# Layer normalisation moved beside a selective scan, one more drive on GpSimd, softplus summed by TensorE

## The chip, the cores and the metric

The kernel runs on one core of a Trainium2 chip. A core has five engines that run side by side, each with its own in-order stream of instructions: TensorE (PE, matrix products), VectorE (DVE), ScalarE (ACT, functions of one value), GpSimd (POOL), and SyncE (SP), which here only issues DMA transfers. They meet through semaphores. The metric is the time of one execution in microseconds on the device, the median of several. The kernel before takes 5625.2 us (three runs, 5623.45 to 5625.22).

## The reference

The input is 8 images of 96 channels and 64 x 64 pixels in float32. Two layers follow each other. The first is a 17 x 17 convolution per channel between two batch normalisations, a 96 x 96 pointwise product, GELU, and a gate per image and channel; its result is added to the input. The second is a bidirectional selective scan (Mamba). Cut to what matters:

```python
h = h * a[:, :, None, None]          # a: gate per image and channel
x = residual + gamma * h             # first layer
# second layer, tokens = the 4096 pixels of an image
mu = xh.mean(-1, keepdims=True); var = xh.var(-1, keepdims=True)
xn = (xh - mu) * rsqrt(var + 1e-05) * ln_g + ln_b
# _mamba, once forward and once over the flipped tokens
x, z = xz[..., :192], xz[..., 192:]  # xz = xn @ W_in
x = silu(causal_conv(x, 4 taps) + conv_b)
proj = x @ W_xproj                   # 6 + 16 + 16 columns
dt = softplus(proj[..., :6] @ W_dt + b_dt)
h = exp(dt * A) * h + dt * B_t * x_t # 192 channels x 16 states
y = sum_s(h * C_t) + x * D
out = (y * silu(z)) @ W_out          # forward + backward
```

## The kernel before

The program has five stages, with a barrier between them: `convolution`, `pointwise` (which leaves the ungated result in DRAM as `act_scr` and the gates in SBUF), `normalise`, `scan` and `output`.

`normalise` works in 64 slices of 512 tokens (8 images, 8 slices each), channels on the 96 partitions. Per slice VectorE makes gate x act + x, TensorE subtracts the mean with a centring matrix, ScalarE squares, TensorE averages, ScalarE makes the reciprocal root with logarithm and exponential, VectorE scales and shifts, and the slice is stored to `xn_scr`.

`scan` goes through 32 iterations of two passes. A pass is one direction of one chunk of 1024 tokens. It has 24 units, each of 128 partitions: 8 channels x 16 states. For a unit, TensorE spreads B over the partitions into one of three PSUM tiles `u_ps` (two bf16 matmuls); VectorE multiplies it by dt x (`u_rep`), the drive; ScalarE makes the decay exp(dt A) from `dt_rep`; VectorE runs the recurrence (`tensor_tensor_scan`) into `hring`; GpSimd multiplies by C into `hc`; TensorE gathers 16 states to a channel in `y_ps`, two units at a time in odd steps. For the units in `POOL_UNITS` GpSimd makes the drive from `u_rep` and `b_rep` into `drive_p`, VectorE does not, TensorE does not spread, and ScalarE puts the decay into the PSUM tile.

A pass has 24 steps, numbered m, and a written table says what each engine does in each step beside the units. The function `run` plays it to each engine in the same order. `front` at step m belongs to unit m + 8 on ScalarE, to unit m + 7 (spread and drive) on TensorE and VectorE, and to unit m + 6 for the scan. The other kinds are: `conv`, the causal convolution for the pass after next, in three groups with a ScalarE copy each (`CONV_AT`); `prep`, for the next pass: SiLU, LOW (the 38 columns of proj, `LOW_AT`), the dt products (`DT_AT`), softplus as relu(v) + ln(1 + exp(-|v|)), u = dt x (`U_AT`), and the stores and loads that replicate dt, u, B and C over the partitions through DRAM; `back`, gather and skip; `gate` and `slice`, which finish one slice of 512 tokens per pass of the image before: z (`Z_AT`), the sum of the two directions in two parts (`SUM_Y_AT`), gating by VectorE, projection (`PROJECT_AT`), result (`RES_AT`). All of conv, prep, gate and slice share one PSUM tile, `prep_ps`, so they follow each other strictly: every product in it waits until the one before is copied out. In softplus the two parts are added by GpSimd (`SUM_AT`), and GpSimd multiplies u.

`output` finishes the last image.

## Time and profile before

| | us |
|---|---|
| median of three runs | 5625.2 |
| the profiled execution | 5622.07 |
| its span, first to last instruction | 5620.2 |
| VectorE busy | 5265.8 (94%) |
| GpSimd busy | 4899.0 (87%) |
| TensorE busy | 4417.3 (79%) |
| ScalarE busy | 3184.7 (57%) |

The stages can be told from the busy time in slices of the span: convolution up to about 340 us, pointwise to 460, `normalise` 460 to 617, `scan` from there to about 5575, then `output`. Lines of the profile are lines of the kernel before: L1419 is the scan, L1401 the drive multiply, L1464 the multiplication by C, L1451 GpSimd's drive, L1170 the spread, L1188 the gather, L1199 the skip, L1211 and L1214 the convolution groups, L1227 and L1230 LOW, L1267 and L1268 the y sum, L1273 and L1274 the projection, L1434 gating, L691 the scaling in `normalise`. A float32 product is recorded as two matmul instructions. The mean of one instruction contains some 0.1 us of overlap with the next one on its engine, so rows in order of time, read from start to start, give what it costs in a dense sequence. TensorE's granted clock (PEclk) is a share of 2.4 GHz and takes two levels, 1.2 and 2.4 GHz, so 0.50 and 1.00.

### The profile page before, as it was taken

How to read it: one execution, taken by the hardware profiler on the slowest of the kernel's cores; microseconds unless marked ns; L12 is line 12 of the kernel's file. 1: busy time of each engine (PE TensorE's matmuls, PEld its weight loads, DVE VectorE, ACT ScalarE, POOL GpSimd, SP SyncE). 2: the span in 40 equal slices, each digit the busy share in tenths (PEclk: the TensorE clock that was granted, in tenths of full speed). 3: DMA queues.
4: the chain of work that ended last, by engine and by line, in shares of the span. 5: the costliest groups of instructions: out<-in, count | busy, mean ns of one | idle time of the engine just before them, and what ended most of it. 6: DMA issues, size and time to landing. Idle time of an engine off the chain costs nothing. (4 is left out here: it accounts for less than half of the span.)

```text
span 5620.2 us, 74988 instructions
## 1 busy us (share of the span) xinstructions
PE 4417.3 (79%) x17412; PEld 1176.0 (21%) x17412; DVE 5265.8 (94%) x3821; ACT 3184.7 (57%) x5221; POOL 4899.0 (87%) x2361
## 2 busy tenths in 40 slices
PE   6878577778878787788887887878778887788887
PEld 4553111111111111111111111111111111111111
DVE  5556499999999999999999999999999999999997
ACT  2237455555555566555666555665555566655564
POOL 0020299999999999999999999999999999999998
PEclk9999776667777777777777777777777777777777
DMA  2238555556656556666656665666665665666666
GB/s 75 76 92 241 164 189 184 186 183 200 212 191 202 196 196 197 207 193 209 191 194 196 204 204 198 196 196 197 202 208 189 206 194 194 198 206 198 205 193 200
DMA packets 365955, 1062.74 MB, mean 189 GB/s; under 512 B 71396, under 2 KB 119926, under 8 KB 315340
## 3 DMA queue, kind: packets, MB, share of 16 engines
q1 hardware_dynamic: 355724, 1045.89, 57.8%
q10 hardware_dynamic: 8064, 14.16, 0.8%
q0 software_dynamic: 1984, 1.06, 0.1%
q14 instruction: 166, 1.36, 0.1%
q8 instruction: 17, 0.28, 0.0%
HBM read 849.20 MB, written 211.63 MB: 189 GB/s over the span
## 5 line engine op out<-in xcount | busy, mean ns | idle before, releaser
L1464 POOL TENSOR_TENSOR hc<-hring,c_rep 128x1024 f32<-128x1024 f32 x1541 | 3599.4, 2358 | 73.1 <-DVE hring L1419 69.6
L1419 DVE TENSOR_TENSOR_SCAN hring<-decay,carry,u_ps 128x1024 f32<-128x1024 f32 x1221 | 2833.8, 2346 | 0.0
L1170 PE MATMUL u_ps<-stack_b,w_spread 48*128 48x512 bf16 x2442 | 992.4, 495 | 1008.6 <-DVE hring L1419 1003.7
L1401 DVE TENSOR_TENSOR u_ps<-u_ps,u_rep 128x1024 f32<-128x1024 f32 x1221 | 1491.7, 1222 | 69.0 <-DMA u_rep<-u_scr 52.9
L1295 ACT ACTIVATE decay<-dt_rep,w_a 128x1024 f32<-128x1024 f32 x1222 | 1396.4, 1145 | 221.2 <-DVE hring L1419 208.1
L1188 PE MATMUL y_ps<-hc,w_gather 128*32 128x512 f32 x6144 | 1131.2, 818 | 0.0
L1295 ACT ACTIVATE u_ps<-dt_rep,w_a 128x1024 f32<-128x1024 f32 x322 | 359.3, 1116 | 1104.2 <-DVE hring L1419 1103.9
L1451 POOL TENSOR_TENSOR drive_p<-u_rep,b_rep 128x1024 f32<-128x1024 f32 x322 | 759.5, 2359 | 10.7 <-DMA u_rep<-u_scr 10.7
L1419 DVE TENSOR_TENSOR_SCAN hring<-u_ps,carry,drive_p 128x1024 f32<-128x1024 f32 x321 | 755.7, 2354 | 0.0
L1170 PEld LDWEIGHTS u_ps<-stack_b,w_spread 48*128 48x128 bf16 x2442 | 144.8, 100 | 2371.0 <-DVE hring L1419 2166.7
L1211 PE MATMUL prep_ps<-xn,w_conv 128*128 128x512 f32 x792 | 476.6, 749 | 27.2 <-DMA xn<-xn_scr 25.5
L1318 ACT ACTIVATE xc<-prep_ps,w_conv_b 128x512 f32<-128x512 f32 x198 | 135.7, 685 | 410.0 <-PE prep_ps L1211 394.8
L322 DVE TENSOR_SCALAR xpad<-xraw,scale,shift 64x128 f32<-64x128 f32 (+1 forms) x600 | 184.0, 359 | 140.9 <-DMA xraw<-in_x_cols 138.1
L367 PE MATMUL pc<-xpad,toep 128*64 128x256 f32 x1920 | 253.7, 410 | 67.1 <-DVE xpad L322 67.1
L233 POOL COPY part<-wide 102x160 bf16 (+1 forms) x26 | 8.9, 343 | 322.9 <-PE pw L346 301.1
L1311 ACT COPY ends<-hring 128x1 f32<-128x1 f32 x1540 | 271.6, 176 | 0.0
L1478 POOL TENSOR_TENSOR b<-b 128x128 f32<-128x128 f32 x65 | 25.7, 395 | 256.8 <-DMA b<-bc_scr 256.8
L1188 PEld LDWEIGHTS y_ps<-hc,w_gather 128*32 128x32 f32 x6144 | 136.1, 122 | 497.8 <-issue 456.0
L1471 POOL TENSOR_TENSOR dt_sb<-soft,dt_sb 128x1024 f32<-128x1024 f32 (+1 forms) x130 | 235.6, 1813 | 3.3 <-ACT soft L1353 3.3
L1475 POOL TENSOR_TENSOR soft<-dt_sb,xa 128x1024 f32<-128x1024 f32 (+1 forms) x130 | 235.1, 1808 | 0.2
L1211 PEld LDWEIGHTS prep_ps<-xn,w_conv 128*128 128x128 f32 x792 | 172.5, 233 | 270.4 <-issue 239.5
L1199 PE MATMUL y_ps<-xa,w_skip 128*32 128x512 f32 (+1 forms) x1536 | 225.0, 662 | 0.0
(148 smaller groups left out, 4044.3 us busy)
## 6 DMA issues: line engine op xcount, KB each, us to landing
dt_rep<-dt_scr SPq DMA_DIRECT2D x194, 1024.0 KB, 5.9
u_rep<-u_scr SPq DMA_DIRECT2D x194, 1024.0 KB, 8.0
c_rep<-bc_scr SPq DMA_DIRECT2D x260, 512.0 KB, 4.9
b_rep<-bc_scr SPq DMA_DIRECT2D x130, 512.0 KB, 4.3
xn<-xn_scr SPq DMA_DIRECT2D x132, 384.0 KB, 5.4
y_scr<-y_sb SPq DMA_DIRECT2D x768, 64.0 KB, 2.0
xn<-xn_scr SPq DMA_DIRECT2D x132, 256.0 KB, 4.7
dt_scr<-dt_sb SPq DMA_DIRECT2D x260, 128.0 KB, 2.1
```

The source lines that it names most:

```text
L367: last = nc.tensor.matmul(pc[c][64 * q:64 * q + 64, 0:B * XH].rearrange("p (f b x) -> p f b x", f=2, b=B), toep[par][:, c * CELLS + k, :], ...
L1170: mm = nc.tensor.matmul(u_ps[nv % NSLOT][:, sl], w["spread"][:, q, :], upper(stack_b[drv][:, sl]), start=True, stop=True)
L1188: last = nc.tensor.matmul(y_ps[at:at + 32, :], w["gather"][:, :], hc[n % NHC][:, i * SL:(i + 1) * SL], start=(q == 0), stop=(q == QN - 1))
L1211: mm = nc.tensor.matmul(prep_ps[:, :], w["conv"][:, j, 0:P], xn[:, j, PART[g]], start=(j == 0), stop=(j == 2))
L1295: nc.scalar.activation(to[:, :], dt_rep[r][:, b, :], ACT.Exp, scale=w["a"][:, col:col + 1]).then_inc(decay_ready, 1)
L1311: nc.scalar.copy(ends[:, drv, nv:nv + 1], hring[nv % NHR][:, end:end + 1]).then_inc(kept, 1)
L1401: nc.vector.tensor_tensor(slot[:, :], slot[:, :], u_rep[r][:, b, :], ALU.mult).then_inc(drive_ready, 1)
L1419: nc.vector.tensor_tensor_scan(hring[nv % NHR][:, ::step], factor[:, ::step], term[:, ::step], carry[:, drv, nv:nv + 1], ALU.mult, ALU.add ...
L1451: nc.gpsimd.tensor_tensor(drive_p[k % 2][:, :], u_rep[r][:, b, :], b_rep[q][:, :], ALU.mult).then_inc(pool_drive, 1)
L1464: nc.gpsimd.tensor_tensor(hc[nv % NHC][:, :], hring[nv % NHR][:, :], c_rep[q][:, :], ALU.mult).then_inc(c_applied, 1)
L1471: nc.gpsimd.tensor_tensor(dt_sb[:, HALVES[h]], soft[:, HALVES[h]], dt_sb[:, HALVES[h]], ALU.add).then_inc(dt_ready, 1)
L1475: nc.gpsimd.tensor_tensor(soft[:, HALVES[h]], dt_sb[:, HALVES[h]], xa[dr][:, HALVES[h]], ALU.mult).then_inc(u_ready, 1)
```

## The change

Three things change.

1. `normalise` only does image 1 (8 slices). Images 2 to 8 are normalised inside `scan`, one slice of 512 tokens per pass, for the image after the one that is scanned (a new kind, `norm`; the last four iterations have none). There the tokens are on the partitions: TensorE centres with the gated centring matrix on act and the plain one on x (8 products of 96 columns), ScalarE squares with a row sum, makes the reciprocal root, scales, TensorE turns the four blocks back, ScalarE applies gain and bias, SP loads and stores. The slice also lives in `prep_ps`, between the result of the step before and the convolution.
2. `POOL_UNITS` has six units in place of five, every fourth.
3. The sum in softplus is made by TensorE with two identity products per part (three parts), and copied back by ScalarE.

The table of steps moves: LOW from 2 to 1, dt from 4, 6, 8 to 3, 4, 5, the convolution groups from 14, 16, 18 to 18, 19, 20, u from 8 and 10 to 10 and 12, z from 20, 22 to 21, 22, the y sums from 0 and 10 to 10 and 12, the projection from 12 to 13. The load of u is issued one step later.

```diff
-POOL_UNITS = (2, 6, 11, 15, 19)
+POOL_UNITS = (2, 6, 10, 14, 18, 22)
...
-                over_slices(sp, (0, load))
+                over_first(sp, (0, load))
...
-        NPREP = 7
+        NPREP = 10
...
-        CONV_AT = ((14, 14, 14), (16, 16, 16), (18, 18, 18))
-        SUM_AT = (7, 9)
-        U_AT = (8, 10)
+        CONV_AT = ((18, 18, 18), (19, 19, 19), (20, 20, 20))
+        SUM_AT = (7, 8, 9)
+        U_AT = (10, 12)
...
+        NORM_IN_AT, NORM_GATE_AT, CENTRE_AT, SQUARE_AT, SCALE_AT, TURN_AT, NORM_OUT_AT, NORM_STORE_AT = 5, 12, 14, 15, 16, 17, 18, 19
...
-                    if n % 8 == 4:
-                        load_u(*later(4, u, n, it, dr))
+                    if n % 8 == 5:
+                        load_u(*later(3, u, n, it, dr))
...
+                def norm(m, p, it, dr, slicing):
+                    if m == NORM_IN_AT:
+                        image, at = norm_slice(it, dr)
+                        free, = ready(p + 1)
+                        sp.wait_ge(centred, free)
+                        sp.dma_start(gate_now[:, :], gate_all[:, bass.ds(image, 1)]).then_inc(norm_in, 16)
+                        sp.dma_start(nh[:, :], d["act_scr"][image, :, bass.ds(at, SL)]).then_inc(norm_in, 16)
+                        sp.dma_start(nx[:, :], d["x_tok"][image, :, bass.ds(at, SL)]).then_inc(norm_in, 16)
+                    if m == NORM_STORE_AT:
...
+                        sp.dma_start(d["xn_scr"][image, :, bass.ds(at + HALO, SL)], nout[:, :]).then_inc(norm_stored, 16)
...
-                            if g == 0 and slicing:
+                            if g == 0 and beside[1]:
+
+                                pe.wait_ge(norm_out, pn - 1)
...
+                    if m in SUM_AT:
+                        g = SUM_AT.index(m)
+                        pe.wait_ge(prep_out, NPREP * pn + 7 + g)
+                        pe.wait_ge(soft_step, 2 * (2 * pn + g // 2) + 2)
+                        nc.tensor.matmul(prep_ps[:, :], w["ident"][:, :], soft[:, PART[g]], start=True, stop=False)
+                        nc.tensor.matmul(prep_ps[:, :], w["ident"][:, :], dt_sb[:, PART[g]], start=False, stop=True).then_inc(prep_done, 1)
...
+                    if m == CENTRE_AT:
+                        pe.wait_ge(norm_in, 48 * (p + 1))
+                        pe.wait_ge(centrer_gated, p + 1)
+
+                        if slicing:
+                            pe.wait_ge(res_ready, p - OUT_LAG + 1)
+                        else:
+                            pe.wait_ge(prep_out, NPREP * (p + 2))
+                        for j in range(NBLK):
+                            to, tok = prep_ps[:, j * C:(j + 1) * C], slice(j * P, (j + 1) * P)
+                            nc.tensor.matmul(to, nh[:, tok], gated_centrer[:, :], start=True, stop=False)
+                            mm = nc.tensor.matmul(to, nx[:, tok], w["centrer"][:, :], start=False, stop=True)
+                        mm.then_inc(centred, 1)
+                    if m == TURN_AT:
+                        pe.wait_ge(tokens_scaled, p + 1)
+                        for j in range(NBLK):
+                            mm = nc.tensor.matmul(prep_ps[0:C, j * P:(j + 1) * P], ntok[:, j, :], w["ident"][:, :], start=True, stop=True)
+                        mm.then_inc(turned_back, 1)
...
+                    if m - 1 in SUM_AT:
+                        g = SUM_AT.index(m - 1)
+                        act.wait_ge(prep_done, NPREP * pn + 8 + g)
+                        nc.scalar.copy(dt_sb[:, PART[g]], prep_ps[:, :]).then_inc(prep_out, 1)
...
+                    if m == SQUARE_AT:
+                        act.wait_ge(turned_back, p + 1)
+                        act.wait_ge(centred, p + 2)
+                        for j in range(NBLK):
+
+                            mm = nc.scalar.activation(ntok[:, j, :], prep_ps[:, j * C:(j + 1) * C], ACT.Square, accum_out=nstat[:, 0, j:j + 1])
+                        mm.then_inc(norm_step, 1)
+                    if m == SCALE_AT:
...
+                        for j in range(NBLK):
+                            mm = nc.scalar.activation(ntok[:, j, :], prep_ps[:, j * C:(j + 1) * C], ACT.Copy, scale=nstat[:, 2, j:j + 1])
+                        mm.then_inc(tokens_scaled, 1)
+                    if m == NORM_OUT_AT:
+                        act.wait_ge(turned_back, p + 2)
+                        act.wait_ge(norm_stored, 16 * (p + 1))
+                        nc.scalar.activation(nout[:, :], prep_ps[0:C, :], ACT.Identity, bias=w["lng"][:, 1:2], scale=w["lng"][:, 0:1]).then_inc(norm_out, 1)
...
-                        if m == SUM_AT[h]:
-                            pool.wait_ge(soft_step, 2 * (2 * pn + h) + 2)
-                            nc.gpsimd.tensor_tensor(dt_sb[:, HALVES[h]], soft[:, HALVES[h]], dt_sb[:, HALVES[h]], ALU.add).then_inc(dt_ready, 1)
                         if m == U_AT[h]:
-                            pool.wait_ge(dt_ready, 2 * pn + h + 1)
+                            pool.wait_ge(prep_out, NPREP * pn + 9 + h)
```

On TensorE the instructions move in three places that matter. The first is the convolution, in the second pass of the last loop. Before, from the second group (`w_conv`, three products of 128 columns' width) to gather and skip (`w_gather`, `w_skip`) of step 19; `w_spread` are the spreads:

```order
L1211 MATMUL prep_ps<-xn,w_conv 128x512 x3
L1165 ISA
L76 REGISTER_ALU
L1170 MATMUL u_ps<-stack_b,w_spread 128x512 x2
L1183 REGISTER_ALU
L1188 MATMUL y_ps<-hc,w_gather 32x512 x4
L76 REGISTER_ALU
L1170 MATMUL u_ps<-stack_b,w_spread 128x512 x2
L76 REGISTER_ALU
L1214 MATMUL prep_ps<-xn,w_conv 64x512 x6
L1188 MATMUL y_ps<-hc,w_gather 32x512 x4
L1199 MATMUL y_ps<-xa,w_skip 32x512 x4
```

Now, from the spread of step 18:

```order
L1232 MATMUL u_ps<-stack_b,w_spread 128x512 x2
L1267 ISA
L1276 MATMUL prep_ps<-xn,w_conv 128x512 x3
L1242 REGISTER_ALU
L1250 MATMUL y_ps<-hc,w_gather 32x512 x4
L1261 MATMUL y_ps<-xa,w_skip 32x512 x4
L76 REGISTER_ALU
L1276 MATMUL prep_ps<-xn,w_conv 128x512 x3
L76 REGISTER_ALU
L1232 MATMUL u_ps<-stack_b,w_spread 128x512 x2
L76 REGISTER_ALU
L1279 MATMUL prep_ps<-xn,w_conv 64x512 x6
```

The second group now stands behind gather and skip in one step, and the third follows after a single spread.

The second place is LOW (`w_low`), at the start of a pass. Before, with the first y sum (`w_ident`) of step 0 ahead:

```order
L1267 MATMUL prep_ps<-y_fwd,w_ident 128x512
L1268 MATMUL prep_ps<-y_bwd,w_ident 128x512
L76 REGISTER_ALU
L1170 MATMUL u_ps<-stack_b,w_spread 128x512 x2
L1180 REGISTER_ALU
L1183 REGISTER_ALU
L1188 MATMUL y_ps<-hc,w_gather 32x512 x4
L76 REGISTER_ALU
L1170 MATMUL u_ps<-stack_b,w_spread 128x512 x2
L1227 MATMUL prep_ps<-xa,w_low 64x512 x2
L1230 MATMUL prep_ps<-xa,w_low 64x512 x2
```

Now, steps 0 to 2:

```order
L76 ISA
L1232 MATMUL u_ps<-stack_b,w_spread 128x512 x2
L76 REGISTER_ALU
L1232 MATMUL u_ps<-stack_b,w_spread 128x512 x2
L1242 REGISTER_ALU
L1245 REGISTER_ALU
L1250 MATMUL y_ps<-hc,w_gather 32x512 x4
L1290 REGISTER_ALU
L1292 MATMUL prep_ps<-xa,w_low 64x512 x2
L1295 MATMUL prep_ps<-xa,w_low 64x512 x2
L76 REGISTER_ALU
L1232 MATMUL u_ps<-stack_b,w_spread 128x512 x2
```

The y sum is gone from here, and a gather stands between the spread and LOW.

The third place is behind the projection (`w_out`). Before, steps 11 to 13:

```order
L1188 MATMUL y_ps<-hc,w_gather 32x512 x4
L1199 MATMUL y_ps<-xa,w_skip 32x512 x4
L1270 REGISTER_ALU
L1273 MATMUL prep_ps<-y_bwd,w_out 96x256
L1274 MATMUL prep_ps<-y_bwd,w_out 96x256
L1273 MATMUL prep_ps<-y_bwd,w_out 96x256
L1274 MATMUL prep_ps<-y_bwd,w_out 96x256
L76 REGISTER_ALU
L1170 MATMUL u_ps<-stack_b,w_spread 128x512 x2
L1188 MATMUL y_ps<-hc,w_gather 32x512 x4
```

Now, steps 13 and 14:

```order
L1342 REGISTER_ALU
L1345 MATMUL prep_ps<-y_bwd,w_out 96x256
L1346 MATMUL prep_ps<-y_bwd,w_out 96x256
L1345 MATMUL prep_ps<-y_bwd,w_out 96x256
L1346 MATMUL prep_ps<-y_bwd,w_out 96x256
L76 REGISTER_ALU
L1232 MATMUL u_ps<-stack_b,w_spread 128x512 x2
L1351 REGISTER_ALU
L1360 MATMUL prep_ps<-gated_centrer,nh 128x96
L1361 MATMUL prep_ps<-w_centrer,nx 128x96
L1360 MATMUL prep_ps<-gated_centrer,nh 128x96
L1361 MATMUL prep_ps<-w_centrer,nx 128x96
```

The projection stands one step later, and the centring (`gated_centrer`, `w_centrer`, the tokens `nh` and `nx` being the loaded operand) follows one spread after it.

## Rows read from the trace of the kernel before

**Rows 1.** Busy time by stage, 1000 to 3000 us: stretch, length, each engine's busy time, clock.

```profile
1000.00:3000.00 2000.00, 1590.87 (x5697) 359.51 (x5698) 1998.97 (x1176) 1186.38 (x1909) 1975.66 (x920) 0.73 0.61 197
```

**Rows 2.** Who waited for whom, 1000 to 5400 us: total us, times, longest.

```profile
DVE u_ps L1401 <- PE u_ps L1170: 2.7, 8, 0.3
```

**Rows 3.** VectorE in order of time, one pass: start us, duration us.

```profile
3016.74 0.41 DVE L1434 TENSOR_TENSOR y_bwd<-prep_ps,z_sb 128x256 f32<-128x256 f32 x1
3017.06 1.23 DVE L1401 TENSOR_TENSOR u_ps<-u_ps,u_rep 128x1024 f32<-128x1024 f32 x1
3018.19 4.58 DVE L1419 TENSOR_TENSOR_SCAN hring<-decay,carry,u_ps 128x1024 f32<-128x1024 f32 x2
3022.68 1.22 DVE L1401 TENSOR_TENSOR u_ps<-u_ps,u_rep 128x1024 f32<-128x1024 f32 x1
...
3092.89 0.41 DVE L1434 TENSOR_TENSOR y_bwd<-prep_ps,z_sb 128x256 f32<-128x256 f32 x1
```

**Rows 4.** VectorE in order of time in `normalise`, scaling of two slices, six apart.

```profile
591.36 0.75 DVE L691 SCALAR_TENSOR_TENSOR xs<-px,lng,rs 96x512 f32<-96x512 f32 x1 [0.33 <-ACT rs L739]
...
604.18 0.75 DVE L691 SCALAR_TENSOR_TENSOR xs<-px,lng,rs 96x512 f32<-96x512 f32 x1 [0.39 <-ACT rs L739]
```

**Rows 5.** GpSimd in order of time.

```profile
3019.55 1.27 POOL L1471 TENSOR_TENSOR dt_sb<-soft,dt_sb 128x512 f32<-128x512 f32 x1
...
3049.87 11.64 POOL L1464 TENSOR_TENSOR hc<-hring,c_rep 128x1024 f32<-128x1024 f32 x5
```

**Rows 6.** SP in order of time, first pass: issue of stores and loads.

```profile
657.10 1.95 SPq L1092 DMA_DIRECT2D u_scr<-soft  x4
...
662.59 0.52 SPq L1013 DMA_DIRECT2D u_rep<-u_scr  x1
```

**Rows 7.** TensorE in order of time, in stretches at full clock.

```profile
3020.59 0.62 PE L1170 MATMUL u_ps<-stack_b,w_spread 48*128 48x512 bf16 x2 [0.20 <-DVE hring L1419]
3021.14 1.06 PE L1188 MATMUL y_ps<-hc,w_gather 128*32 128x512 f32 x8
...
3030.12 2.84 PE L1211 MATMUL prep_ps<-xn,w_conv 128*128 128x512 f32 x6
...
3061.98 1.08 PE L1227 MATMUL prep_ps<-xa,w_low 128*64 128x512 f32 x4
```

**Rows 8.** TensorE in order of time, wholly or partly at half clock.

```profile
3008.87 1.93 PE L1188 MATMUL y_ps<-hc,w_gather 128*32 128x512 f32 x8
3010.74 1.03 PE L1170 MATMUL u_ps<-stack_b,w_spread 48*128 48x512 bf16 x2
...
3018.23 0.87 PE L1273 MATMUL prep_ps<-y_bwd,w_out 128*96 128x256 f32 x2
3018.94 0.59 PE L1274 MATMUL prep_ps<-y_bwd,w_out 128*96 128x256 f32 x2
...
3056.36 2.07 PE L1267 MATMUL prep_ps<-y_fwd,w_ident 128*128 128x512 f32 x2
...
3106.28 4.40 PE L1211 MATMUL prep_ps<-xn,w_conv 128*128 128x512 f32 x6
```

**Rows 9.** Busy time by short stretches, columns as in rows 1.

```profile
2999.40:3006.10 6.70, 6.70 (x17) 1.06 (x16) 6.70 (x5) 4.58 (x7) 6.62 (x6) 0.50 0.22 54
...
3020.60:3045.80 25.20, 19.10 (x82) 4.84 (x82) 25.20 (x15) 13.38 (x23) 25.20 (x13) 1.00 0.71 235
```

**Rows 10.** TensorE's weight loads in order of time, 128 columns.

```profile
627.40 0.34 PEld L1211 LDWEIGHTS prep_ps<-xn,w_conv 128*128 128x128 f32 x1 [0.52 <-issue]
...
632.42 0.19 PEld L1211 LDWEIGHTS prep_ps<-xn,w_conv 128*128 128x128 f32 x1 [0.24 <-issue]
```

**Rows 11.** ScalarE in order of time: a decay and a copy out of PSUM.

```profile
3053.41 1.15 ACT L1295 ACTIVATE decay<-dt_rep,w_a 128x1024 f32<-128x1024 f32 x1
...
3054.54 0.58 ACT L1362 COPY y_sb<-y_ps 128x512 f32<-128x512 f32 x1
```

**Rows 12.** Loads of u, 1000 to 5400 us.

```profile
DMA to landing us min/median/max: 5.6/8.0/11.3
```

144 lines of the change are left out of this document (98 added, 46 removed).

## The prediction

> **What bounds the kernel now.** I read the busy time by stage first, then who waited for whom, then VectorE's instructions in order of time, and last TensorE's. From 1000 us on VectorE is busy all the time, 1998.97 of 2000 us, and GpSimd 1975.66 [rows 1]. The waits agree: VectorE waited 2.7 us in all, for TensorE [rows 2]. So VectorE sets the pace and every microsecond in which it has nothing ready is added to the end.
>
> One pass (24 units of one direction and one chunk) is the step from one small gating multiply to the next, 3016.74 to 3092.89, 76.15 us [rows 3]. Two scans in a row take 4.49 us from start to start (3018.19 to 22.68), 2.245 each, and a drive multiply 1.12 (3017.06 to 3018.19). 24 x 2.245 + 19 x 1.12 is 75.2, and the two gating multiplies are the other 0.9: the pass is the sum of its instructions. There are 64 passes. The rest of the span lies around them: the normalisation, the first preparation and the output. The profiled run took 5622.1 us in all against a span of 5620.2; the median is 3.1 above it.
>
> **1. Normalisation of images 2 to 8 leaves its stage.** That stage works slice by slice. Six slices take 604.18 - 591.36 = 12.82 us, 2.137 each [rows 4]. 56 of 64 slices go: -119.7 us. Filling and draining the pipeline stay. The halo writes, whose first bytes follow the eight loads, lie beside the drain. This term is the surest one.
>
> **2. One drive per pass goes to GpSimd.** VectorE loses 1.12 us per pass: 64 x 1.12 = -71.7 us, if nothing makes it wait. GpSimd gets one multiply (five take 11.64, 2.32 each) and loses the two softplus additions, one like it and one of 1.27, 1.23 without its overlap [rows 5]. Its work per pass was 1975.66 / 2000 x 76.15 = 75.2 us and becomes 75.2 + 2.32 - 3.55 = 74.0. VectorE's becomes 75.0. GpSimd stays just below it, so I cost it at nothing; if that cover went, the pass could be no shorter than its 74.0 plus what it waits.
>
> **3. The start of the first pass gets longer.** u was ready when its store was issued, at 657.10, and u_rep was issued at 662.59 [rows 6]. Two GpSimd operations of 2.34 us stood between the logarithm and u. Now three sums on TensorE follow the last Relu: the first at half clock 3.5 us (as the pair of the y sum, 2 x 2.07 less overlap and a clock rise at its end [rows 8]), a ScalarE copy of 0.6, the next 1.9 to 3.5, another copy, then u (2.34). It is ready 6 to 7 us later. Both stores of step 12 (four issues, 1.95 us each) also stand ahead of the first load. Bounds 4 and 12, I take +7 us.
>
> **4. TensorE, in order, between two deadlines.** ScalarE has room: 57% busy, and three copies, nine small activations and one of 96x512 add about 6 us of 75. TensorE is another matter. A spread needs the PSUM slot that the scan three units earlier frees, and its drive multiply follows one scan (and one drive) later. So each spread has one step of VectorE, 3.365 us (2.245 where the drive is GpSimd's), from its release to its deadline, and whatever TensorE does after the spread before must fit in. I count a pass's time from its step 0 as VectorE would run it without waits: step 13 starts at 41.3, 14 at 44.65, 16 at 50.3, 17 at 53.6, 18 at 57.0, 20 at 62.6. The release comes with the scan's end, 0.16 us after VectorE's next start (the scan of 3018.19 ends at 3020.54, the spread starts at 3020.59 [rows 3, 7]). I price each block twice, start to start: at full clock a spread is 0.55 (0.62 to its end), a gather pair 1.0, a skip the same, a convolution group 2.82 [rows 7]; at half clock 0.96 (1.03), 1.87, 1.87, and the group 4.4 where the clock rose on the way [rows 8]. The granted clock was 0.50 in one stretch of a pass and 1.00 in another [rows 9].
>
> (a) Steps 18 to 20. Before, the three groups stood at steps 14, 16 and 18, with only a spread or a gather between. Now they stand at 18, 19 and 20, and step 19 also has gather and skip. From the release of the spread of step 18 to the deadline of that of step 20 VectorE needs 3.365 + 3.365 + 2.245 = 8.98 us. At full clock TensorE needs 0.16 + 0.55 + 2.82 + 1.0 + 1.0 + 2.82 + 0.62 = 8.97. It just fits, if the group starts at once. It does not: it waits for ScalarE's norm_out. In the pass's time the second gating ends at 41.4, the projection at 43.2, its copy at 43.85, the centring at 46.9 (c); a decay is 1.15 us and a 512-wide copy 0.58 [rows 11]; four squares with row sums I estimate at 1.6, logarithm, exponential and four scalings at 1.5, by the copy's size, so decay, y copy and these end at 51.9. The turn ends at 52.9, two decays at 54.2, norm_out at 54.9, where TensorE could have begun at 54.35: 0.6 late. With the turn and the start of the group at half clock it is 3.2 late. I take 1.1 per pass, nearer the full clock, which held over the groups in the trace [rows 9].
> (b) Step 1. LOW stood at step 2, without a gather, at full clock (1.08 + 1.07) behind the 512-wide y sum of step 0. That sum is now at step 10. Spread, gather, LOW, spread at half clock: 0.16 + 0.96 + 1.87 + 4.2 (twice 2.1) + 1.03 = 8.2 against 6.73. Late by 0 to 1.5; I take 0.3, since a group that began at half clock took 4.40 and not twice 2.82 [rows 8].
> (c) Steps 13 to 16. The projection waits for the second gating multiply, now at step 12. At full clock, 0.43 for each of four pairs (0.59 less the overlap), 0.16 + 1.75 + 0.62 fits in 3.365. At half clock, 0.71 per pair (3018.23 to 18.94 [rows 8]), it is 0.7 late. Then come 16 matmul instructions of 96 columns for the centring, each with its own load of 128 columns. The trace has none of this shape; the nearest are weight loads of 0.19 at full and 0.34 us at the other clock [rows 10], so 3.0 to 5.4 us. With res copy 0.6, gather and spread the chain is 7.1 to 12.0 against 8.98: 0 to 3.0 late. I take 0.8, in the 56 passes that have it. The page "TensorE: Matmul & The Clock Gate" of the Trainium skill (section on LDWEIGHTS) has a load last its columns divided by 1.2 GHz; an estimate by that page is 16 x 0.107 = 1.7 us, and nothing would be late here. The rows of the trace are longer, and I keep them.
> (d) Steps 7 to 9, the three sums: 1.9 each at full clock, 3.5 at half. The first has a pool step before it and fits; the others follow it on a raised clock. 0, at most 1.0.
>
> Waits in all: 56 x 0.8 + 64 x (1.1 + 0.3) = 134 us. Bounds: 3 us (only (a) at 0.05) and 469 us (56 x 3.0 + 64 x 4.7).
>
> **5. DMA.** The loads and stores of the normalisation move beside the scan, three loads and a store per pass of 192 KB on the one queue of SP. The u store waits one step longer and u_rep is issued from step 13: GpSimd takes up unit 15 with the end of its scan at 31.5 us of the pass and has u at 36.5; eight store issues and their landing put the load's issue at about 42, and it lands 5.6 to 11.3 us later, by the median 8.0 [rows 12], so at 50 to 53.4; the deadline is 53.6. No wait, but the margin is a third of a microsecond at its longest.
>
> **Sum.** 5622.1 - 119.7 - 71.7 + 7 + 134 = 5571.7; with 3.1 to the median 5575 us.
>
> **The rivals.**
> A. TensorE stays on time. For it: the clock was 1.00 from 3020.6 to 3045.8 with convolution groups in it [rows 9]. Against: 8.97 of 8.98 leaves nothing for ScalarE's chain. Time: 5622.1 - 119.7 - 71.7 + 7 + 3 + 3.1 = 5444. The page "TensorE: Matmul & The Clock Gate" of the Trainium skill (section "Why this matters for your kernels") says that work without gaps holds the full clock; by it the added work would pay for itself and this would be the case. The trace disagrees in part: from 2999.4 to 3006.1 TensorE was busy 6.70 of 6.70 us at 0.50 [rows 9], and the y sum of 3056.36 still ran at half clock [rows 8].
> B. TensorE becomes the bound, the slower side. Its busy time is 1590.87 of 2000 us already [rows 1], 60 us per pass, and sums (5.7 at full clock), centring and turn (4) come on top of it, less one spread. Place: the spreads of steps 16 and 20 at half clock. With (a) 2.5, (b) 0.75 and (c) 1.5 late: 64 x 3.25 + 56 x 1.5 = 292, so 5575 - 134 + 292 = 5733. It decides from waits of (119.7 + 71.7 - 7 - 3.1) / 64, some 2.8 us per pass on; my own value is 2.1, so it is not far.
> C. The u_rep loads land late. For it the thin margin above; against it that any wait in steps 13 to 16 widens it. Two microseconds per pass on top: 5575 + 128 = 5703.
> D. The normalisation's chain (load, centre, store) delays the convolution's input: stores are issued at step 19, the next image's first input is read at step 0. Five steps for about 4 us: unlikely, and no price beyond a few microseconds at each of 7 image changes.
>
> **Chances.** A measurement here tells a change from none at about 0.2%, 11 us. Mine, with waits of 0.8 to 2.7 us per pass, has 0.46 (own range 5495 to 5613). A has 0.15. Waits about where B begins to decide, 2.7 to 3.0 us, give no change, 0.11. B beyond that has 0.25, C (with D) 0.03. So faster 0.61, same 0.11, slower 0.28. The range for 8 in 10 is 5450 to 5695.
>
> **What will show it.** The normalisation stage is 8 slices, some 35 us instead of 155. Steps of the pass: VectorE's idle before the drive multiply, put down to TensorE's u_ps, was 2.7 us and should be 100 to 180 us, most of it before the drives of units 3, 21 or 23, and 9. If it is under 20 us, A holds and the pass is 75.0. If the idle is put down to u_rep's DMA, C. Scans keep 2.35 us. TensorE's busy share rises to 85 to 90% with a granted clock above 0.75; if the clock is lower than before, B. The weight loads of the centring tell 0.19 from 0.34. I am wrong in kind if GpSimd or ScalarE is what VectorE waits for.

## The result, and the profile after

The changed kernel takes 5650.06 us (median of six runs, 5647.07 to 5651.88) against 5624.27 us for the kernel before on the same chip: ratio 1.0046, 95% interval 1.0033 to 1.0058. It is slower by half a per cent, by the interval clear of no change; 5575 was forecast, 0.9% faster. The profiled run's span is 5646.9 us (5620.2 before), with a mean granted clock of 0.811 (0.753).

Busy time of each engine after, as in [rows 1]:

```profile
1000.00:3000.00 2000.00, 1680.45 (x6418) 492.88 (x6418) 1918.29 (x1116) 1279.27 (x2335) 1889.84 (x867) 0.81 0.63 201
```

VectorE is idle for 81.7 of 2000 us where it was idle for 1. Who waited for whom (1000 to 5000 us; total, times, longest), as in [rows 2]:

```profile
DVE u_ps L1526 <- PE u_ps L1232: 142.7, 116, 4.0
...
POOL hc L1589 <- PE y_ps L1250: 109.6, 93, 2.4
...
DVE hring L1544 <- issue: 9.9, 23, 0.7
```

VectorE waits for TensorE's spread, as the forecast named it. GpSimd waits for a gather of TensorE as well; no row puts a wait of VectorE down to GpSimd. The last row is the scan of unit 6, in 23 passes, every second one: as often as the loop of 24 iterations (`Fori` in L1009) jumps back, and at that place. GpSimd's drive for this scan had ended 12 to 14 us before; what the scan waits for is not shown.

The normalisation and the start of the first pass, VectorE and GpSimd with TensorE's first softplus sum between, in order of time:

```profile
459.51 0.75 DVE L693 SCALAR_TENSOR_TENSOR x<-h_in,gate,x_in_ln 96x512 f32<-96x512 f32 x1 [2.47 <-DMA x_in_ln<-in_x_tok]
...
485.41 0.10 DVE L1508 MEMSET ends<- 128x48 f32 x1 [3.09 <-PEq L658]
...
524.89 2.07 PE L1313 MATMUL prep_ps<-soft,w_ident 128*128 128x512 f32 x2 [1.36 <-ACT dt_sb L1440]
...
536.49 1.26 POOL L1597 TENSOR_TENSOR soft<-dt_sb,xa 128x512 f32<-128x512 f32 x1 [0.32 <-ACT dt_sb L1449]
...
551.28 2.34 DVE L1544 TENSOR_TENSOR_SCAN hring<-decay,carry,u_ps 128x1024 f32<-128x1024 f32 x1
```

The first normalised slice to the scan's memset is 25.9 us; it was 617.32 - 467.06 = 150.3. The memset to the first scan is 65.9 us; it was 672.63 - 617.32 = 55.3. The books on the two spans: stages ahead of the normalisation -7.5, normalisation -124.4, start +10.6, first scan to the end 4947.6 to 5095.6, +148.0; sum +26.7. The forecast had +62.7 for the last term (134 of waits less 71.7 of drives): the waits are some 219 us, 3.4 per pass, 85 more than the forecast's 134.

Where in the pass they stand (mean over all passes, idle time of VectorE before the instruction, summed from its rows in order of time; later means have the same base where no other is named): before the drive of unit 3 (step 20) 2.07 us, of unit 21 0.36, of unit 23 0.34, the scan of unit 6 0.15, the drives of units 4 and 9 0.09 and 0.05. That is 3.1; the rest is the overlap of 0.1 to 0.2 us that two instructions lose at each stop. The wait before unit 3 has two sizes. A pass of the one kind, TensorE's rows and the drive at the end:

```profile
2984.83 2.02 PE L1366 MATMUL prep_ps<-w_ident,ntok 128*96 128x128 f32 x8
...
2987.89 2.81 PE L1276 MATMUL prep_ps<-xn,w_conv 128*128 128x512 f32 x6 [0.27 <-ACT nout L1499]
2990.63 1.07 PE L1250 MATMUL y_ps<-hc,w_gather 128*32 128x512 f32 x8
2991.63 1.06 PE L1261 MATMUL y_ps<-xa,w_skip 64*32 64x512 f32 x8
2992.62 2.84 PE L1276 MATMUL prep_ps<-xn,w_conv 128*128 128x512 f32 x6
2995.40 0.62 PE L1232 MATMUL u_ps<-stack_b,w_spread 48*128 48x512 bf16 x2
2996.05 1.23 DVE L1526 TENSOR_TENSOR u_ps<-u_ps,u_rep 128x1024 f32<-128x1024 f32 x1 [0.93 <-PE u_ps L1232]
```

And one of the other, and its granted clock (the third number from the end) before and behind the middle of the stretch:

```profile
3768.90 2.02 PE L1366 MATMUL prep_ps<-w_ident,ntok 128*96 128x128 f32 x8
...
3771.96 4.70 PE L1276 MATMUL prep_ps<-xn,w_conv 128*128 128x512 f32 x6
3776.59 1.07 PE L1250 MATMUL y_ps<-hc,w_gather 128*32 128x512 f32 x8
...
3781.36 0.62 PE L1232 MATMUL u_ps<-stack_b,w_spread 48*128 48x512 bf16 x2
3782.01 1.23 DVE L1526 TENSOR_TENSOR u_ps<-u_ps,u_rep 128x1024 f32<-128x1024 f32 x1 [3.65 <-PE u_ps L1232]
```

```profile
3766.10:3775.00 8.90, 8.82 (x24) 3.62 (x25) 8.90 (x6) 4.22 (x7) 8.90 (x5) 0.50 0.81 227
3776.60:3782.00 5.40, 5.37 (x25) 1.47 (x24) 1.76 (x1) 2.34 (x4) 4.25 (x3) 1.00 1.00 331
```

The reader is to see that the same first group takes 2.81 us on the full clock (2.4 GHz) and 4.70 when most of it runs on the half clock (1.2 GHz). The waits at the end differ by 2.72 us: 1.89 of it is the group, the other 0.83 lies ahead of the turn (L1366). Of the 56 passes with normalisation 39 are of the first kind, with a mean wait of 1.26 us, and 17 of the second, with 3.70. In the last 8 passes, without normalisation, the group is on the half clock too, with 2.3 to 2.9. The turn is on the half clock in the first kind as well, 2.02 us in both cuts: of 56 turns none ran on the full clock from end to end, 39 ran wholly on the half clock.

Projection, spread and centring of step 14, and the drive of unit 21:

```profile
2975.99 1.03 PE L1232 MATMUL u_ps<-stack_b,w_spread 48*128 48x512 bf16 x2
2976.95 0.49 PE L1360 MATMUL prep_ps<-gated_centrer,nh 96*128 96x96 f32 x2
...
2977.06 1.23 DVE L1526 TENSOR_TENSOR u_ps<-u_ps,u_rep 128x1024 f32<-128x1024 f32 x1 [0.77 <-PE u_ps L1232]
...
2978.62 0.39 PE L1361 MATMUL prep_ps<-w_centrer,nx 96*128 96x96 f32 x2
```

Eight pairs follow each other every 0.22 us here. In 36 of the 56 passes they follow every 0.43 us. The two places are not independent: where centring ran on the half clock, the first group was on the full clock in 30 of 36 passes; where centring ran on the full clock, in 9 of 20 only.

### The profile page after: what moved, and what is told of

The parts are those of the page before. It is cut to its first block and busy times, and to the rows that moved or that the text cites. A ratio compares the mean times of both kernels' runs of the same rounds, so it can differ in the third digit from the quotient of the medians.

```text
span 5646.9 us, 79806 instructions
## 1 busy us (share of the span) xinstructions
PE 4651.8 (82%) x19184; PEld 1479.2 (26%) x19184; DVE 5119.6 (91%) x3592; ACT 3394.3 (60%) x6144; POOL 4830.5 (86%) x2295
## 5 line engine op out<-in xcount | busy, mean ns | idle before, releaser
L1544 DVE TENSOR_TENSOR_SCAN hring<-decay,carry,u_ps 128x1024 f32<-128x1024 f32 x1157 | 2673.4, 2335 | 0.0
L1526 DVE TENSOR_TENSOR u_ps<-u_ps,u_rep 128x1024 f32<-128x1024 f32 x1157 | 1405.1, 1215 | 264.2 <-PE u_ps L1232 193.8
L1387 ACT ACTIVATE decay<-dt_rep,w_a 128x1024 f32<-128x1024 f32 x1158 | 1326.1, 1148 | 174.7 <-DVE hring L1544 165.1
L1232 PE MATMUL u_ps<-stack_b,w_spread 48*128 48x512 bf16 x2314 | 870.5, 464 | 645.7 <-DVE hring L1544 641.8
L1576 POOL TENSOR_TENSOR drive_p<-u_rep,b_rep 128x1024 f32<-128x1024 f32 x386 | 912.6, 2364 | 11.2 <-DMA u_rep<-u_scr 11.2
L1544 DVE TENSOR_TENSOR_SCAN hring<-u_ps,carry,drive_p 128x1024 f32<-128x1024 f32 x385 | 902.1, 2343 | 9.9 <-issue 9.9
L1387 ACT ACTIVATE u_ps<-dt_rep,w_a 128x1024 f32<-128x1024 f32 x386 | 430.7, 1116 | 369.7 <-DVE hring L1544 368.4
L1313 PE MATMUL prep_ps<-soft,w_ident 128*128 128x512 f32 x390 | 280.1, 807 | 10.5 <-ACT dt_sb L1440 1.4
L1449 ACT COPY dt_sb<-prep_ps 128x512 f32<-128x512 f32 x195 | 114.3, 586 | 212.1 <-PE prep_ps L1314 211.5
L1314 PE MATMUL prep_ps<-dt_sb,w_ident 128*128 128x512 f32 x390 | 213.8, 630 | 0.0
```

Source lines behind the costliest of these rows:

```text
L1232: mm = nc.tensor.matmul(u_ps[nv % NSLOT][:, sl], w["spread"][:, q, :], upper(stack_b[drv][:, sl]), start=True, stop=True)
L1313: nc.tensor.matmul(prep_ps[:, :], w["ident"][:, :], soft[:, PART[g]], start=True, stop=False)
L1387: nc.scalar.activation(to[:, :], dt_rep[r][:, b, :], ACT.Exp, scale=w["a"][:, col:col + 1]).then_inc(decay_ready, 1)
L1526: nc.vector.tensor_tensor(slot[:, :], slot[:, :], u_rep[r][:, b, :], ALU.mult).then_inc(drive_ready, 1)
L1544: nc.vector.tensor_tensor_scan(hring[nv % NHR][:, ::step], factor[:, ::step], term[:, ::step], carry[:, drv, nv:nv + 1], ALU.mult, ALU.add ...
L1576: nc.gpsimd.tensor_tensor(drive_p[k % 2][:, :], u_rep[r][:, b, :], b_rep[q][:, :], ALU.mult).then_inc(pool_drive, 1)
```

## The experiments

Theory 1 (the clock): the spreads are late because TensorE enters the dense stretches (projection and centring, turn and groups) on the half clock, and it does so because it was idle shortly before. Theory 2 (the load): there is simply too much TensorE work between release and deadline. Theory 3 (the chain): ScalarE's squares and norm_out hold up the first group. A table first; the waits are VectorE's for u_ps in 1000 to 5000 us (some 51 to 53 passes), the clock is that of the same stretch, the ratio is to the kernel before.

| kernel | us | ratio (95%) | waits | clock |
|---|---|---|---|---|
| before | 5624 to 5627 | 1 | 2.4 | 0.73 |
| changed | 5650.1 | 1.0046 (1.0033 to 1.0058) | 142.7 | 0.81 |
| E1 before, groups at 18, 19, 20 | 5778.0 | 1.0270 (1.0253 to 1.0287) | 109.8 | 0.73 |
| E2 before, groups at 18, 20, 21 | 5754.8 | 1.0228 (1.0212 to 1.0243) | 106.2 | 0.69 |
| E3 before, sixth drive | 5713.2 | 1.0157 (1.0140 to 1.0174) | 0 | 0.74 |
| E4 changed, normalised ahead | 5764.7 | 1.0246 (1.0229 to 1.0263) | 156.0 | 0.80 |
| E5 changed, sums on GpSimd | 5645.4 | 1.0037 (1.0024 to 1.0050) | 143.4 | 0.74 |
| E6 changed, products at 16, 17 | 5603.7 | 0.9964 (0.9942 to 0.9986) | 102.4 | 0.85 |
| E7 changed, spaced | 5570.5 | 0.9903 (0.9887 to 0.9920) | 101.9 | 0.80 |
| E8 E7, projection at 14 | 5586.9 | 0.9920 (0.9900 to 0.9941) | 136.7 | 0.79 |
| E9 E8, products at 13, 14 | 5487.6 | 0.9750 (0.9734 to 0.9766) | 32.5 | 0.87 |
| E10 E7, product at 13 | 5522.4 | 0.9816 (0.9800 to 0.9832) | 60.1 | 0.84 |
| E11 E8, products at 12, 13, 14 | 5484.8 | 0.9747 (0.9731 to 0.9764) | 25.4 | 0.87 |
| E12 E7, products at 12, 13, 17 | 5547.1 | 0.9850 (0.9833 to 0.9866) | 78.4 | 0.85 |
| E13 changed, products at 12, 13, 14 | 5585.8 | 0.9925 (0.9910 to 0.9940) | 87.3 | 0.85 |
| E14 E13, projection at 14, product at 17 too | 5568.6 | 0.9898 (0.9883 to 0.9913) | 63.9 | 0.87 |
| E15 E11, product at 17 too | 5487.5 | 0.9755 (0.9742 to 0.9768) | 20.2 | 0.88 |

A "product" is one matrix product of 128 x 512 columns into the PSUM slot that the spread behind it overwrites; nobody reads it.

**E1. Adjacent groups alone, in the kernel before.**

```
-        CONV_AT = ((14, 14, 14), (16, 16, 16), (18, 18, 18))
-        SLICE_AT, Z_AT = 15, (20, 22)
+        CONV_AT = ((18, 18, 18), (19, 19, 19), (20, 20, 20))
+        SLICE_AT, Z_AT = 15, (21, 22)
```

> The kernel before with one part of the change only: the three convolution groups at steps 18, 19 and 20 and z at 21 and 22. No normalisation in the scan, softplus sums on GpSimd, five drives there. Theory (the adjacent groups cost by themselves): a wait before the drive of unit 3 of 0.5 to 1.5 us per pass, since its own spread must share 8.98 us (the drive of unit 2 is GpSimd's, that of unit 3 VectorE's) with 8.97 us of TensorE work at full clock and more at half: 5624 + 64 x (0.5 to 1.5) = 5656 to 5720, I take 5680. Rival (only with the normalisation's chain does it cost): wait under 0.1 us, 5624 to 5632.

5778.0 us, +152 where +56 was taken, and above the whole range given. TensorE and VectorE at the place:

```profile
3038.78 1.03 PE L1170 MATMUL u_ps<-stack_b,w_spread 48*128 48x512 bf16 x2 [0.48 <-DVE hring L1419]
3039.74 4.65 PE L1211 MATMUL prep_ps<-xn,w_conv 128*128 128x512 f32 x6
...
3049.08 0.62 PE L1170 MATMUL u_ps<-stack_b,w_spread 48*128 48x512 bf16 x2
3049.74 1.23 DVE L1401 TENSOR_TENSOR u_ps<-u_ps,u_rep 128x1024 f32<-128x1024 f32 x1 [2.04 <-PE u_ps L1170]
```

There is no normalisation and no chain of ScalarE here, and the group starts behind its spread at once. With the groups gone from steps 14 and 16 TensorE is idle there between spreads (2.75 and 2.34 us before two of them), and the first group starts on the half clock (0.50 granted from 3035.5 to 3043), in all 64 passes. In the kernel before, the first group (step 14) took over 3 us in 36 of 64 passes, the second in 18 and the third in 19, and VectorE waited 2.7 us in all [rows 2]. So the half clock alone is no delay: it takes a deadline close behind. This one part of the change costs 2.4 us per pass by itself, and Theory 3 is not needed for it.

**E2. Groups one step apart, in the kernel before.** `CONV_AT = ((18, 18, 18), (20, 20, 20), (21, 21, 21))`, z at 21 and 22.

> The kernel before with its three convolution groups at steps 18, 20 and 21 (instead of 14, 16 and 18) and z at 21 and 22, nothing else. If only two groups with gather and skip between them cost: 5624 to 5635, against 5778 with the groups at 18, 19 and 20. If a long stretch without groups before step 18 and the half clock that follows it cost by themselves: a wait of 0.5 us or more per pass, 5656 or more.

5754.8 us: the second case, and more of it. The wait has moved to the drive of unit 5 and has its old size:

```profile
3014.37 4.85 PE L1211 MATMUL prep_ps<-xn,w_conv 128*128 128x512 f32 x6
...
3030.66 0.62 PE L1170 MATMUL u_ps<-stack_b,w_spread 48*128 48x512 bf16 x2
3031.31 1.23 DVE L1401 TENSOR_TENSOR u_ps<-u_ps,u_rep 128x1024 f32<-128x1024 f32 x1 [2.25 <-PE u_ps L1170]
```

Again a first group of 4.85 us on the half clock, in all 64 passes, and the spread of step 22 now stands behind a group and a z product. Placement alone does not mend it.

**E3. The sixth drive alone, in the kernel before.** `POOL_UNITS = (2, 6, 11, 15, 19, 22)`, `B_AT = (11, 13)`.

> The kernel before with only a sixth drive on GpSimd (unit 22 beside 2, 6, 11, 15, 19), the softplus additions staying on GpSimd. VectorE has 75.0 us of work per pass, GpSimd 75.2 + 2.32 = 77.5. Theory (GpSimd becomes the bound): pass 77.5 to 78.3 us instead of 76.15, 5624 + 64 x (1.4 to 2.1) = 5714 to 5758, I take 5725, with VectorE's idle put down to GpSimd. Rival (GpSimd's overlaps and its idle share hide it): 5553, the 71.7 us gained.

5713.2 us, a microsecond under the range given, pass 77.48. VectorE's wait in 1000 to 5000 us:

```profile
DVE hring L1419 <- POOL hc L1464: 115.6, 54, 2.4
```

GpSimd's work of 77.5 us, summed from its rows, is the pass to 0.1 us. In this kernel the sixth drive gains nothing while the additions stay on GpSimd.

**E4. All images normalised ahead of the scan,** the rest as changed (on all four engines of the stage, and no normalisation tasks in the scan):

```
-                over_first(sp, (0, load))
+                over_slices(sp, (0, load))
...
-                iteration(it, (True, True), (True, True), True)
+                iteration(it, (True, True), (True, True), False)
```

> The changed kernel with all eight images normalised before the scan, and no normalisation tasks beside it; softplus sums on TensorE, six drives and the convolution's steps stay. Expected of every theory: about +124 us in the normalise stage. Theory (adjacent groups are enough for most of the wait, the normalisation's chain adds the rest): the wait before the drive of unit 3 falls from 2.07 to about 0.6 to 1.0 us per pass (only the late start of the group and the half clock of the turn go), the one before unit 23 (0.34) goes: 5650 + 124 - 64 x (1.2 + 0.35) = 5675 (5650 to 5700). Rival (norm_out alone makes the spread late): the wait before unit 3 is under 0.2: 5650 + 124 - 64 x 2.4 = 5620. Rival (the clock: fewer columns on TensorE, lower clock): waits grow: over 5774.

5764.7 us, 114.6 above the changed kernel (which gives back 124.4 in its stage). The normalisation beside the scan costs it, on balance, only some 10 us; a longer wait without it, next, is part of this balance. The wait before unit 3 is not smaller without it, but 2.76 us in the mean:

```profile
3022.71 5.49 PE L1273 MATMUL prep_ps<-xn,w_conv 128*128 128x512 f32 x6
...
3033.55 1.23 DVE L1523 TENSOR_TENSOR u_ps<-u_ps,u_rep 128x1024 f32<-128x1024 f32 x1 [2.88 <-PE u_ps L1229]
```

With centring and turn gone the first group starts on the half clock in all 64 passes and stays there nearly to its end (5.4 to 5.5 us) in 60, where the changed kernel has 25 such starts of 64. All three prices were missed; the direction (less work, a slower group, a longer wait) is that of the third. So the load of centring and turn does not make this wait, nor does ScalarE's chain, which is gone here. What both do once the clock is up, E4 can't tell; E14 comes back to it.

**E5. Softplus's additions back on GpSimd,** six drives and all else as changed. The products and copies of steps 7 to 10 go, and on GpSimd stands

```
+                        if m == (7, 9)[h]:
+                            pool.wait_ge(soft_step, 2 * (2 * pn + h) + 2)
+                            nc.gpsimd.tensor_tensor(dt_sb[:, HALVES[h]], soft[:, HALVES[h]], dt_sb[:, HALVES[h]], ALU.add).then_inc(dt_ready, 1)
```

> The changed kernel with softplus's additions back on GpSimd (two instead of three products and copies on TensorE and ScalarE), six drives on GpSimd, everything else as changed. GpSimd has 74.0 + 3.55 = 77.5 us of work per pass. Theory (TensorE's waits in steps 16 to 20 hardly depend on the sums of steps 7 to 9, and GpSimd has 78.6 us per pass in the changed kernel): 5640 to 5665 if the GpSimd work fits into the waits that are there, more if its lateness adds to them: 5690 at most; I take 5660. Rival (the sums cost TensorE what VectorE waits for): 5600 or less.

5645.4 us, the interval overlaps that of the changed kernel. As long as TensorE's waits make the pass 78.6 us, 77.5 us of GpSimd's work fit in, and moving the sums brings nothing. The mean clock is 0.74 here against 0.81, at the same time: what counts is the clock where a deadline is near (first group not on the full clock in 29 passes here, in 25 there).

**E6. Two products of idle work, in steps 16 and 17 of the changed kernel.**

```
+                    if nv in FILL:      # FILL = (0, 23)
+                        nc.tensor.matmul(u_ps[nv % NSLOT][:, 0:SL], w["ident"][:, :], <512 columns of w["conv"]>, start=True, stop=True)
                     for i in range(2):  # the spread
```

> The changed kernel with one more product of 512 columns on TensorE in steps 20 and 17 of each pass (ahead of the spreads of units 23 and 0 of each pass, identity times weights into the PSUM slot that the spread then overwrites; its result is not used). Theory 1 (the half clock before the turn and the first convolution group makes the wait): with more work ahead the clock is up earlier, the turn takes 1.1 instead of 2.0 us in more passes and the wait before unit 3 shrinks from 2.07 to about 1.2: 5650 - 55 = 5595. Theory 2 (the load in the stretch makes it): each product adds 0.2 to 0.43 us ahead of a spread: the wait before units 3, 0 or 23 grows by 0.2 to 0.4 us: 5663 to 5676. If neither counts, 5650.

(The spreads of units 23 and 0 are issued in steps 16 and 17, not 20 and 17.) 5603.7 us, with a spread of 5582.8 to 5626.1 over its six runs, wider than in any other kernel but one. In the following cut the clock is up ahead of the turn:

```profile
2957.54 1.11 PE L1369 MATMUL prep_ps<-w_ident,ntok 128*96 128x128 f32 x8
...
2959.70 2.81 PE L1279 MATMUL prep_ps<-xn,w_conv 128*128 128x512 f32 x6 [0.49 <-ACT nout L1502]
...
2967.86 1.23 DVE L1529 TENSOR_TENSOR u_ps<-u_ps,u_rep 128x1024 f32<-128x1024 f32 x1 [0.62 <-PE u_ps L1235]
```

46 us less by adding work: Theory 1. Turn and first group are on the full clock in 50 of 56 passes, and there the wait before unit 3 is 0.54 us; in the mean over all passes it is 0.97 instead of 2.07. Part of it is given back: the waits before units 23 and 21 rise from 0.34 and 0.36 to 0.60 and 0.47.

**E1 with three products** in steps 15, 16 and 17 (`FILL = (0, 22, 23)`).

> The kernel before with the adjacent groups (as in the last of the first four runs, 5778 us) and one more product of 512 columns, whose result is not used, ahead of the spreads of units 22, 23 and 0 (steps 15, 16 and 17), where TensorE is idle for 0.5 to 2.3 us per step. Theory (the wait before the drive of unit 3 is there because the first group starts on a half clock: 4.65 us instead of 2.8): with TensorE busy ahead of step 18 the group runs at full clock and the wait of 2.04 to 2.15 us per pass falls below 0.3: 5778 - 64 x 2.3 = 5630 (5622 to 5660). Rival (sheer work between release and deadline; a further 0.9 to 1.9 us of work in each of three steps can only delay): 5778 or more, up to 5900.

Three of four runs took 5763 to 5766 us and one 5664, so there is no verdict on its time. The profiled run is one of the three:

```profile
3025.70 0.62 PE L1173 MATMUL u_ps<-stack_b,w_spread 48*128 48x512 bf16 x2
3026.25 2.84 PE L1214 MATMUL prep_ps<-xn,w_conv 128*128 128x512 f32 x6
...
3033.79 0.62 PE L1173 MATMUL u_ps<-stack_b,w_spread 48*128 48x512 bf16 x2
3034.45 1.23 DVE L1404 TENSOR_TENSOR u_ps<-u_ps,u_rep 128x1024 f32<-128x1024 f32 x1 [0.71 <-PE u_ps L1173]
```

The group does run on the full clock, in all 64 passes, and the wait before unit 3 falls from 2.14 to 0.66. But the products themselves ran on the half clock (2.08 us each), which made the spread of unit 23 1.2 us late and TensorE come to step 18 with a backlog. On the full clock the stretch from spread to spread takes 3034.41 - 3025.70 = 8.71 us: close to the 8.97 of the forecast, with no room for a late start. The run of 5664 us was not profiled, and no conclusion rests on this kernel.

**E7. Groups at 18, 20, 21 in the changed kernel,** z at 22 and 23, its second copy one step later still.

```
-        CONV_AT = ((18, 18, 18), (19, 19, 19), (20, 20, 20))
-        SLICE_AT, Z_AT = 15, (21, 22)
+        CONV_AT = ((18, 18, 18), (20, 20, 20), (21, 21, 21))
+        SLICE_AT, Z_AT = 15, (22, 23)
```

> The changed kernel with its second and third convolution group one step later (steps 18, 20, 21), so that the gather and skip of step 19 no longer share one release-to-deadline stretch with two groups; the z products move to steps 22 and 23 and the second z copy to the next pass's step 0. Theory (adjacent groups): the wait before the drive of unit 3, 2.07 us per pass, goes nearly whole (to under 0.4), and the pass falls from 79.6 to about 77.3 us, so about 5650 - 64 x 2.2 = 5509 us (5490 to 5540). Rival 1 (the chain through ScalarE's norm_out is what makes the spread late): the first group of step 18 still begins late, and the wait stays at 1 us or more per pass before units 1 to 3: 5580 or more. Rival 2 (TensorE as a whole is the bound): the wait appears elsewhere, before units 4 to 6 or 9, with the same sum, and the time stays within 10 us of 5650.

5570.5 us: 80 less, not 140, which is in none of the three ranges. The wait before unit 3 is 0.26, as the theory of adjacent groups had it, but that before unit 21 rose from 0.36 to 0.94, and one of 0.21 came before unit 5:

```profile
3084.09 1.17 PE L1345 MATMUL prep_ps<-y_bwd,w_out 128*96 128x256 f32 x2 [2.06 <-DVE y_bwd L1559]
...
3087.75 1.03 PE L1232 MATMUL u_ps<-stack_b,w_spread 48*128 48x512 bf16 x2
...
3088.82 1.23 DVE L1526 TENSOR_TENSOR u_ps<-u_ps,u_rep 128x1024 f32<-128x1024 f32 x1 [1.40 <-PE u_ps L1232]
```

The projection stands idle for 2.06 us until the gating multiply is done, and then starts on the half clock; it takes 3.2 to 3.7 us in all 56 passes, where one on the full clock takes 1.97 (17 of 56 in the changed kernel). The spread behind it waits.

**E8. The projection behind the spread of step 14.** In TensorE's code `if m == PROJECT_AT + 1:`.

> The spaced kernel (groups at steps 18, 20, 21) with TensorE's projection issued in step 14 instead of 13, that is behind the spread of unit 21 instead of ahead of it. The projection waits for the second gating multiply either way. Theory (at half clock the projection of 3.1 to 3.9 us stands between the release of that spread and its deadline): the wait before the drive of unit 21, 0.94 us per pass, goes, and that before unit 23 (0.28) goes in part, since the projection starts the spread's 0.6 to 1.0 us later but the spread behind it is gone: 5570 - 64 x (0.9 to 1.3) = 5487 to 5512, I take 5500. Rival (TensorE as a whole is the bound, and a wait taken away comes back at another place of the pass): the idle time of VectorE stays about 2 us per pass, 5560 to 5575.

5586.9 us (5568.6 to 5595.2): no gain, and above the rival's range too. The wait before unit 21 is gone and stands before unit 23, 2.30 us in the mean from 1000 to 5000 us (1.87 over all passes):

```profile
3021.72 1.17 PE L1345 MATMUL prep_ps<-y_bwd,w_out 128*96 128x256 f32 x2
...
3026.29 0.71 PE L1360 MATMUL prep_ps<-gated_centrer,nh 96*128 96x96 f32 x2 [0.84 <-ACT res L1473]
...
3031.79 1.89 PE L1232 MATMUL u_ps<-stack_b,w_spread 48*128 48x512 bf16 x4
...
3032.86 1.23 DVE L1526 TENSOR_TENSOR u_ps<-u_ps,u_rep 128x1024 f32<-128x1024 f32 x1 [2.85 <-PE u_ps L1232]
```

The rival looked right here. But it leaves open why: the whole stretch is on the half clock, and centring is in 50 of 56 passes.

**E9. E8 with products ahead of the spreads of steps 13 and 14,** where TensorE had nothing to do (`FILL = (20, 21)`).

> The spaced kernel with the projection in step 14 (5587 us) and one more product of 512 columns, whose result is not used, ahead of the spreads of units 20 and 21 (steps 13 and 14), where TensorE is idle for 1.1 and 1.8 us while it waits for VectorE. Clock theory: projection and centring ran at half clock (3.5 and 3.4 us) because TensorE was idle in steps 11 to 14; with these gaps filled they take 1.8 each in most passes, the wait before unit 23 (2.30 us per pass) falls under 0.5: 5587 - 64 x 1.9 = 5465 (5450 to 5500). Load theory: two products add 0.9 to 2.1 us each ahead of a spread, and the wait stays or grows: 5587 to 5650. Lock theory (a pass settles at 78.51 us whatever makes it wait): no change, 5580 to 5595.

5487.6 us, 99 less than E8, and the same place reads:

```profile
3058.67 1.13 PE L1232 MATMUL u_ps<-w_conv,w_ident 128*128 128x512 f32 x2 [0.70 <-DVE hring L1547]
3059.73 0.62 PE L1235 MATMUL u_ps<-stack_b,w_spread 48*128 48x512 bf16 x2
3060.28 0.67 PE L1348 MATMUL prep_ps<-y_bwd,w_out 128*96 128x256 f32 x2
...
3063.10 0.43 PE L1363 MATMUL prep_ps<-gated_centrer,nh 96*128 96x96 f32 x2 [0.85 <-ACT res L1476]
```

The projection is on the full clock in all 56 passes and centring in 55. Two products more of TensorE work per pass, and its busy time in 1000 to 5000 us fell from 3491 to 3415 us. At this place the load theory and a fixed pass length both fall.

**E10 to E12. Other places for products.** E7 with one in step 13:

> The spaced kernel (projection in step 13, 5570 us) with one such product ahead of the spread of unit 20 alone (step 13). TensorE then still has up to 1 us of idle time before the second gating multiply. Clock theory: half the projections run at full clock, the wait before unit 21 falls from 0.94 to about 0.5: 5540 (5500 to 5560). Load theory: 5570 or more.

E8 with three, in steps 12, 13 and 14:

> As the first of these four, with a third product ahead of the spread of unit 19 (step 12), so that TensorE has hardly an idle microsecond from step 11 on. Clock theory: as good as the first or better, 5450 to 5480. Load theory: 64 x 0.9 to 2.1 us of work more than that, 5600 to 5700.

E7 with three, in steps 12, 13 and 17:

> The spaced kernel (projection in step 13) with such products ahead of the spreads of units 19, 20 and 0 (steps 12, 13 and 17): the clock raised for the projection and again for the turn and the first group. Clock theory: waits before units 21 and 3 go in most passes: 5460 to 5520. Load theory: 5600 or more.

5522.4, 5484.8 and 5547.1 us. The first lies in the clock's range: 55 of 56 projections were on the full clock, not half of them. The second is the fastest here, together with E9, and 5 us above the range it was given. The third did not reach the clock's range: there is a wait before unit 1 now (0.31 us from 1000 to 5000 us), and units 3 and 5 kept 0.5 each. Two products were added there against E10, so the 25 us between them are not put down to one; the wait before unit 1 stands right behind the product of step 17.

**E13 to E15. How the 2.1 us divide.** The changed kernel with the products of steps 12 to 14; that with the projection at 14 and a product at 17 too; and the same with spaced groups:

> The changed kernel (adjacent groups, projection in step 13) with three products of 512 columns, whose results are not used, ahead of the spreads of units 19, 20 and 21 (steps 12 to 14). Clock theory: the waits before units 21 and 23 (0.36 and 0.34 us per pass) go or are replaced by the product that now stands between projection and spread of unit 21, and the chain to norm_out gets 1.6 us shorter, so that the first group starts earlier; the wait before unit 3 falls from 2.1 to about 1.0: 5650 - 64 x 1.5 = 5555 (5530 to 5600). Load theory: 5650 or more.

> The changed kernel with adjacent groups, the projection in step 14 and four such products, ahead of the spreads of units 19, 20, 21 and 0 (steps 12, 13, 14 and 17). At full clock TensorE needs 8.7 to 9.0 us of the 8.98 between the release of the spread of step 18 and the deadline of that of step 20, and starts 0.6 us late by ScalarE's chain and the turn. If the clock made the whole rest: wait before unit 3 of 0.5 to 0.9 us per pass, 5444 + 64 x 0.9 = about 5500 (5480 to 5530). If adjacency costs much even at full clock: 1.5 us per pass or more, 5550 or more.

> Spaced groups, projection in step 14 and four such products (steps 12, 13, 14 and 17): the best version so far (5485) with the clock held for the turn and the first group too. Its remaining waits are 0.63 us per pass. If the clock makes them: 5455 to 5475. If the fourth product only loads TensorE ahead of the turn: 5490 to 5520, with a wait before unit 1 of up to 0.3 us per pass as in the version with products in steps 12, 13 and 17.

5585.8, 5568.6 and 5487.5 us. The first lies in the clock's range, but not by its reason: the wait before unit 3 is 1.78 us (1.0 was taken), and the first group is on the half clock in 30 of 56 passes, more than the 17 of the changed kernel. Projection and centring have the full clock now, and a later place has it less often. The gain comes from the waits before units 21 and 23, 0.70 us together before and 0.19 now, and from an earlier start of the groups that are on the full clock.

The last two differ by the steps of the groups and of z alone, at a mean clock of 0.87 and 0.88: 81 us, 1.27 per pass. But a mean clock hides what the clock is at the place. A pass of E14 with everything on the full clock:

```profile
3025.87 1.11 PE L1369 MATMUL prep_ps<-w_ident,ntok 128*96 128x128 f32 x8
...
3028.03 2.81 PE L1279 MATMUL prep_ps<-xn,w_conv 128*128 128x512 f32 x6 [0.49 <-ACT nout L1502]
...
3036.19 1.23 DVE L1529 TENSOR_TENSOR u_ps<-u_ps,u_rep 128x1024 f32<-128x1024 f32 x1 [0.63 <-PE u_ps L1235]
```

Turn and first group are on the full clock in 38 of its 64 passes, with a mean wait of 0.63 us before unit 3. In 18 the turn is not (2.49 us), and in the 8 without normalisation the group is not (3.14). So adjacency with ScalarE's chain costs some 0.6 us per pass, an estimate of 40 us over 64 passes from these rows, once the clock is really up; the 0.49 us that the group waits for norm_out is Theory 3's share of it. The rest of the 81 us still belongs to the half clock. The changed kernel lies another 81 us above E14: that is the half clock and the projection's place together, which no run separates. In the third the fourth product adds nothing to E11.

The best version, E11, is faster than the kernel before by 2.5% (ratio 0.9747, 0.9731 to 0.9764) and than the changed kernel by 2.9% (5484.8 to 5650.1).

## Why the prediction was wrong

*Step 1, normalisation:* right, -124.4 for -119.7. E4 adds that its work beside the scan costs some 10 us on balance.

*Step 2, one drive less:* right. GpSimd at 74.0 us does not bound the pass; its sum of 77.5 for the case without the moved additions is measured in E3. The GpSimd waits that came (for TensorE's gathers) were not foreseen, and no row shows that they cost VectorE anything. Not foreseen either is the wait at the loop's jump, 0.15 us per pass.

*Step 3, start:* +10.6 for +7, within its bounds. Two of three sums ran on the half clock, not one.

*Step 4a, adjacent groups:* this is the step that failed, by its size. The place (unit 3) was right, and so was the price on the full clock: 0.6 late by the forecast, 0.54 and 0.63 in the passes of E6 and E14 in which turn and first group are on the full clock. The changed kernel has no such pass. With the turn on the half clock and the group on the full it is 1.26 late (39 passes), with the group on the half clock too 3.70 (17 passes; 3.2 by the forecast). What failed was "I take 1.1 per pass, nearer the full clock, which held over the groups in the trace [rows 9]". It held over the groups of the one pass that was read. In that trace the first group was on the half clock in 36 of 64 passes, the second in 18, and the 4.40 us of [rows 8] that the forecast uses is such a second group. There a slow group had room and cost nothing; at steps 18 to 20 it has none. E1 shows the cost without any other part of the change, and there the gap that the groups leave at steps 14 and 16 puts the first one on the half clock in all passes.

In numbers: the mean is 2.07 us instead of 1.1, some 62 us over 64 passes, of the 75 by which the forecast was off. The forecast's own two prices with the split that came (39 passes and 25) give 0.6 x 39 + 3.2 x 25 = 103 us for its 70, so about half of the miss is the choice between them, and the other half the case between the two, which had no price. The overlap lost at each stop (some 20 us) and the scan of unit 6 (10) had no term either; LOW, the earlier stages and the normalisation came out 28 us lower together and give most of this back.

*Step 4b, LOW:* 0.05 for 0.3. *Step 4c:* the waits before units 21 and 23 are 0.70 us over 64 passes, which is 0.8 in the 56 that have them, as forecast. But the price of centring was too high at both levels, 3.0 and 5.4 us, so the wait came out right partly by luck: measured were 2.0 us on the full clock and 3.7 on the half, which 36 of 56 passes had. The page "TensorE: Matmul & The Clock Gate" of the Trainium skill (section on LDWEIGHTS) gave an estimate of 1.7 us. The trace agrees on the full clock, an instruction every 0.11 us; on the half clock it is one every 0.21. *Step 4d:* no wait at the sums, as taken. *Step 5, DMA:* no wait; rivals C and D did not come.

*Rival A* needed the full clock everywhere, and its 5444 us was reached by no run. E14, with the groups as changed and the clock raised by products, has 5568.6 and still waits 0.63 us before unit 3 in its best passes. *Rival B* is what happened in its mild form: it gave 2.8 us per pass as the point from which it decides, and 3.4 came; its 5733 us was too much. But its reason, that TensorE is full, is wrong. The changed kernel's clock rose (0.81 for 0.73), TensorE was busy 82% of the span, and more work made it faster.

The page "TensorE: Matmul & The Clock Gate" of the Trainium skill (section "Why this matters for your kernels") says that work without gaps holds the full clock. The forecast weighed this in rival A and did not draw the other side from it, that moved blocks leave gaps. E9 agrees with the page: with the gaps of steps 13 and 14 filled, 56 of 56 projections are on the full clock (2 of 56 in E8).

## What to carry to other kernels

An engine whose speed depends on what it did just before has no fixed price per operation: price a dense block at the clock of the stretch ahead of it in the new order, not in the old one. Do not take that clock from one pass: count over all passes how often the block runs at each level (36, 18 and 19 of 64 slow here, where the pass that was read showed none). A slow block that costs nothing where it has room costs its whole excess where a deadline stands close behind. Blocks that are moved together also leave a gap, and the first of them then stands behind it (E1). If a deadline is missed on the half clock while TensorE is idle a few steps earlier, filling that gap with unused products can be worth more than moving anything: 99 us here for two (E8 to E9). Look at every place afterwards: raising the clock at one can leave a later one with less of it (E13).

## What had not been expected of the hardware

Five kernels with waits at different places settle to the same pass: E1 and the same with products (waits before units 3, and 23 and 3), E2 (unit 5), E4 (unit 3) and E8 (unit 23) all repeat at 78.50 to 78.51 us for dozens of passes, though VectorE's work is 75.0 us in two of them (E4, E8) and up to 76.1 in the others. In the changed kernel the passes vary, for long stretches a shorter and a longer one in turn, between 77.5 and 79.7 us (from one scan of unit 8 to the next, passes 10 to 50); in E7 between 76.7 and 79.0. The clock's changes and the pass seem to fall into step with each other; no run here tells by what rule, and this stays open. In E2 and E8 a wait taken away at one place came back at another; whether this locking is the reason is not shown.
